# Last attention: the causal mask moves from TensorE to VectorE, rows over two PSUM banks, columns over two

## What is computed

```
def _L3_attn_ref(x, W1, b1, W2, b2):
    B, S, E = x.shape
    y = jnp.einsum('bse,ef->bsf', x, W1) + b1
    y = y.reshape(B, S, H, -1).transpose(0, 2, 1, 3)
    q, k, v = jnp.split(y, 3, axis=-1)
    w = jnp.einsum('bhqd,bhkd->bhqk', q, k) / dk
    mask = jnp.tril(jnp.ones((S, S), dtype=x.dtype))
    w = w * mask - NEG_BIG * (1.0 - mask)
    w = jax.nn.softmax(w, axis=-1)
    attn = jnp.einsum('bhqk,bhkd->bhqd', w, v)
...
    return jnp.einsum('bse,ef->bsf', attn, W2) + b2
```

## Time and profile before

| | |
|---|---|
| median of 3 runs | 1892.53 us (1886.91 to 1892.79) |
| profiled execution | 1895.08 us, its span 1893.3 us |
| busy TensorE, weight load, VectorE, ScalarE, GpSimd | 88, 73, 71, 58, 57% of the span |
| row maxima of the last attention that go into XNT (L2193) | 256, mean 502 ns |
| mean granted TensorE clock | 0.947 of full speed |

### The profile page before, as it was taken

How to read it: one execution, slowest core, us unless ns; L and a number is a source line. 1 busy time by engine, 2 the same in 40 slices (tenths; PEclk the granted TensorE clock), 3 DMA queues, 4 the chain that set the end, 5 groups by cost and what they waited for, 6 DMA issues and landing times. The chain is left out here.

```text
span 1893.3 us, 33635 instructions
## 1 busy us (share of the span) xinstructions
PE 1666.8 (88%) x12948; PEld 1385.3 (73%) x12976; DVE 1335.2 (71%) x2744; ACT 1090.4 (58%) x2240; POOL 1081.8 (57%) x1029
## 2 busy tenths in 40 slices
PE   6999999999999999999956888955898468999997
PEld 4888888888888888877855677844687356666676
DVE  6888888888888888743363477677577588777772
ACT  3677776667676767654544555632433345666666
POOL 4888899999999999980054455644177510101011
PEclk9999999999999999999968999966999788999999
DMA  3000000000100000000014200030165200000000
GB/s 93 15 1 15 1 6 10 2 15 1 38 1 1 2 1 1 1 28 0 1 56 141 71 11 2 2 95 0 35 149 129 54 1 1 1 2 2 1 2 24
DMA packets 57839, 47.92 MB, mean 25 GB/s; under 512 B 8384, under 2 KB 49504, under 8 KB 57552
## 3 DMA queue, kind: packets, MB, share of 16 engines
q1 hardware_dynamic: 48128, 32.92, 5.9%
q0 software_dynamic: 8496, 12.33, 3.0%
q10 hardware_dynamic: 1056, 0.52, 0.1%
HBM read 36.45 MB, written 9.31 MB: 24 GB/s over the span
## 5 line engine op out<-in xcount | busy, mean ns | idle before, releaser
L750 POOL TENSOR_TENSOR dtl<-dts,dth 128x512 fp32r<-128x512 f32 x256 | 350.1, 1368 | 20.5
L680 DVE TENSOR_REDUCE nm<-PS 128x1 f32<-128x1024 f32 x256 | 311.3, 1216 | 24.3 <-PE PS L200 23.1
L2032 ACT ACTIVATE ET_a<-PS 128x256 f32<-128x256 f32 (+2 forms) x512 | 222.6, 493 | 125.5 <-PE PS L1945 78.8
L748 POOL CAST dth<-dts 128x512 fp32r<-128x512 f32 x256 | 237.1, 926 | 52.8 <-ACT dts L607 51.7
L198 PE MATMUL PS<-xh,yh 128*128 128x512 f32 x512 | 225.2, 440 | 10.5 <-ACT XNT L600 5.3
L1843 POOL TENSOR_SCALAR_AFFINE_SELECT ET_a<-ET_a 128x1024 f32<-128x1024 f32 x32 | 34.9, 1092 | 310.4 <-ACT ET_a L2032 310.4
L141 PE MATMUL PS<-C,XN 128*128 128x128 f32 x1120 | 176.4, 283 | 38.3 <-POOL W4h L1121 22.7
L200 PE MATMUL PS<-xh,yl 128*128 128x512 f32 x512 | 204.2, 399 | 0.0
L199 PE MATMUL PS<-xl,yh 128*128 128x512 f32 x512 | 204.0, 398 | 0.0
L600 ACT ACTIVATE XNT<-PS,nm 128x1024 f32<-128x1024 f32 x128 | 142.7, 1115 | 80.9 <-DVE nm L680 80.2
L607 ACT ACTIVATE dts<-PS 128x512 f32<-128x512 f32 x256 | 152.5, 597 | 46.7 <-POOL dtl L750 44.0
(11 more groups left out here) (430 smaller groups left out, 4378.3 us busy)
## 6 DMA issues: line engine op xcount, KB each, us to landing
e_wg<-in_WgT SPq DMA_DIRECT2D x16, 256.0 KB
e_wu<-in_WuT SPq DMA_DIRECT2D x16, 256.0 KB
e_wd<-in_WdT SPq DMA_DIRECT2D x16, 256.0 KB
m_x_rows<-m_xs SPq DMA_DIRECT2D x1, 1472.0 KB, 5.1
m_xs<-m_x_rows SPq DMA_DIRECT2D x5, 256.0 KB
m_y_rows<-m_xs SPq DMA_DIRECT2D x5, 256.0 KB, 2.8
X<-in_L_attn_X SPq DMA_DIRECT2D x2, 512.0 KB, 4.6
wqn<-in_L_attn_Wq SPq DMA_DIRECT2D x8, 128.0 KB, 2.1
```

Of the source, the lines that this page charges most:

```text
L680: e.tensor_reduce(self.nm[:, half, i:i + 1], self.S[half], AX.X, MAX, negate=True).then_inc(*self.top.up((g, half)))
L748: e.tensor_copy(hi, src).then_inc(*ts.up((g, g4, "h")))
L750: e.tensor_tensor(lo, src, f(hi), SUB).then_inc(*ts.up((g, g4, "l")))
L2032: e.activation(dst, src, ACT.Exp, scale=self.SC, bias=0.0).then_inc(*self.ex.up(it))
```

## The change

The mask is no longer added by matmuls. GpSimd makes a bf16 tile `mk` of 1024 columns, zero but for the causal block in its last 128. For each query tile VectorE runs one `tensor_tensor_reduce` over 128 to 1024 columns: it adds the last columns of `mk` to the scores, multiplies by -1, writes the result back to PSUM and takes the minimum, that is the negated maximum. The instruction is followed by an accumulator read of 128x1. Tiles 4 to 7 lie in two neighbouring banks, filled by two matmuls of up to 512 columns (the second of 256 at least), and `P2` and the joining minimum go. Row tiles stand at places 0, 1, 2, 3, 4, 6, 8, 10 instead of 0 to 11. Tiles 0 to 3 use banks 0 to 3, tiles 4 to 7 the pairs 0-1 and 2-3 in turn, in all heads; columns use banks 4 and 5 while there are rows. A part waits for the readers of all its banks.

```
-        self.at = {(3 * j if kind == 1 else j): j for j in range(self.nr)}
+        self.col_at = {(3 * j if kind == 1 else j): j for j in range(self.nc_)}
+        self.row_at = {3 * j: j for j in range(4)} if kind == 1 else dict(zip((0, 1, 2, 3, 4, 6, 8, 10), range(8)))
...
-        rs, cs, rn, cn = list(range(3 if kind == 1 else 6)), [], 0, 0
+        rs, cs, rn, cn = [0, 1, 2], [], 0, 0
...
+        def put(it, banks):
+            self.bank_of[it] = banks[0], len(banks)
+            self.before[it] = [u for u in dict.fromkeys(last.get(b) for b in banks) if u]
+            for b in banks:
+                last[b] = it
         for x in range(NH + 8):
             if x == 5:
-                rs, cs, rn, cn = [0, 1, 2], [3, 4, 5], 0, 0
+                cs, rn, cn = [4, 5] if kind == 3 else [3, 4, 5], 0, 0
             elif x == NH:
                 cs, cn = list(range(4)), 0
...
+                    if kind == 3:
+                        put(it, [j] if j < 4 else [2 * (j % 2), 2 * (j % 2) + 1])
...
             if self.kind == 3:
-                i, c0, c1, first = self.rparts[j]
-                wd = max(c1 - c0, 256)
-                t = e.matmul(o[:, 0:wd], qs[:, 128 * i:128 * i + 128], kh[:, c0:c0 + wd], start=True, stop=first)
-                if not first:
-                    t = e.matmul(o[:, c1 - c0 - 128:c1 - c0], w.identb[:, :], w.mk[:, 0, 0:128], start=False, stop=True)
+                for c0 in range(0, 128 * j + 128, 512):
+                    wd = max(min(128 * j + 128 - c0, 512), 256)
+                    t = e.matmul(o[:, c0:c0 + wd], qs[:, 128 * j:128 * j + 128], kh[:, c0:c0 + wd], start=True, stop=True)
...
-                i, c0, c1, first = self.rparts[j]
-                dst = self.P2[:, n % 2, i - 4, hh:hh + 1] if first else M[:, i, col]
-                e.tensor_reduce(dst, o[:, 0:c1 - c0], AX.X, MAX, negate=True).then_inc(*self.top.up(it))
-                if j == self.nr - 1:
-                    m4 = M[:, 4:8, col].rearrange("p i c -> p (i c)")
-                    q.wait_ge(self.top, it)
-                    e.tensor_tensor(m4, m4, self.P2[:, n % 2, :, hh], MIN).then_inc(*self.top.up(("both", x)))
+                if j == 0:
+                    q.wait_ge(w.ready, "mask")
+                wd = 128 * j + 128
+                e.tensor_tensor_reduce(out=o[:, 0:wd], in0=o[:, 0:wd], in1=w.mk[:, 1024 - wd:1024], scale=-1.0, scalar=3e38, op0=ADD, op1=MIN,
+                                       accum_out=M[:, j, col]).then_inc(*self.top.up(it))
...
-            e.tensor_copy(self.mk[:, 0, 0:128], k.cst("caus")).then_inc(*ready.up("mask"))
+            e.memset(self.mk[:, 0:896], 0.0).then_inc(*ready.up("open"))
+            e.tensor_copy(self.mk[:, 896:1024], k.cst("caus")).then_inc(*ready.up("mask"))
```

More of the change, by code:

```diff
@@ L1088, in __init__ @@
         ops += ["one"] if kind == 3 else ["bq0", "one"]
-        ops += [("bm", 0), ("bm", 1), "ident"] + ([("mask", i, j) for i in range(3) for j in range(2)] if kind == 1 else ["mask"]) + ["va1", "va0"]
+        ops += [("bm", 0), ("bm", 1)] + (["ident"] + [("mask", i, j) for i in range(3) for j in range(2)] if kind == 1 else ["open", "mask"]) + ["va1", "va0"]
         self.ready = k.sig("s_weights", ops)
@@ L1629, in __init__ @@
         if kind == 3:
-            self.rparts, self.cparts = [], []
+            self.cparts = []
             for i in range(8):
-                w_ = 128 * (i + 1)
-                cut = 0 if w_ <= 512 else (384 if w_ == 640 else 512)
-                self.rparts += [(i, 0, cut, True)] * (cut > 0) + [(i, cut, w_, False)]
                 lo = 128 * i
@@ L1639, in __init__ @@
         else:
-            self.rparts, self.cparts = list(range(4)), list(range(4))
-        self.nr, self.nc_ = len(self.rparts), len(self.cparts)
+            self.cparts = list(range(4))
+        self.nr, self.nc_ = 8 if kind == 3 else 4, len(self.cparts)
         self.avs = [self.av_of(x) for x in range(NH)]
@@ L1688, in __init__ @@
         last = {b: first[b] for b in range(3 if kind == 1 else 4)}
-        rs, cs, rn, cn = list(range(3 if kind == 1 else 6)), [], 0, 0
+        rs, cs, rn, cn = [0, 1, 2], [], 0, 0
         rows, cols = [], []
+        def put(it, banks):
[3 more added lines that the diff above has]
+                last[b] = it
         for x in range(NH + 8):
             if x == 5:
-                rs, cs, rn, cn = [0, 1, 2], [3, 4, 5], 0, 0
+                cs, rn, cn = [4, 5] if kind == 3 else [3, 4, 5], 0, 0
             elif x == NH:
                 cs, cn = list(range(4)), 0
[L1696 to L1699, removed]
-                    cols.append(it)
-                if x < NH:
-                    b, rn, it = rs[rn % len(rs)], rn + 1, ("row", x, self.at[place])
-                    self.bank_of[it], self.before[it], last[b] = b, last.get(b), it
+            for place in range(14):
+                if place in self.col_at and 0 <= x - 5 < NH:
+                    it = ("col", x - 5, self.col_at[place])
+                    put(it, [cs[cn % len(cs)]])
+                    cn += 1
+                    cols.append(it)
+                if place in self.row_at and x < NH:
+                    it, j = ("row", x, self.row_at[place]), self.row_at[place]
+                    if kind == 3:
+                        put(it, [j] if j < 4 else [2 * (j % 2), 2 * (j % 2) + 1])
+                    else:
+                        put(it, [rs[rn % 3]])
+                    rn += 1
                     rows.append(it)
@@ L1733, in __init__ @@
         self.row = k.sig("a_row", rows)
-        self.top = k.sig("a_row_max", [y for r in rows for y in ([r] + ([("both", r[1])] if kind == 3 and r[2] == self.nr - 1 else []))])
+        self.top = k.sig("a_row_max", rows)
         self.col = k.sig("a_col", cols)
@@ L1792, in bank_free @@
     def bank_free(self, q, it):
[L1793 to L1802, removed]
+        for a in self.before[it]:
+            if a[0] == "project":
+                q.wait_ge(self.mi, a)
+            elif a[0] == "row":
+                q.wait_ge(self.top, a)
+            else:
+                q.wait_ge(self.ex, a)
+        return self.k.bank(*self.bank_of[it])
     def steps(self):
@@ L1867, in maxima @@
             _, n, c = u
-            q.wait_ge(self.top, ("both", 4 * n + 3) if self.kind == 3 else ("row", 4 * n + 3, self.nr - 1))
+            q.wait_ge(self.top, ("row", 4 * n + 3, self.nr - 1))
             for j in range(4):
@@ L1975, in pe @@
                 self.moe.pe_at(e, q, x, j, self)
[L1976 to L1979, removed]
+            if j in self.col_at and 0 <= x - 5 < self.NH:
+                col(x - 5, self.col_at[j])
+            if j in self.row_at and x < self.NH:
+                row(x, self.row_at[j])
             if j in self.AV_AT and 0 <= x - 6 < self.NH:
@@ L2017, in col @@
             it = ("col", x, j)
-            o = k.bank(self.bank_of[it])
+            o = k.bank(*self.bank_of[it])
             if x >= 2:
@@ L2207, in dve @@
         for x, j in self.steps():
-            if j in self.at and x < self.NH:
-                row(x, self.at[j])
+            if j in self.row_at and x < self.NH:
+                row(x, self.row_at[j])
             if (x, j) in self.misc:
```

10 lines of the change are left out of this document (5 added, 5 removed).

## The result

Over four runs of each the median went from 1891.86 us (1886.91 to 1892.79) to 1922.65 us (1918.76 to 1925.23). The ratio is 1.017, with a 95% interval of 1.0156 to 1.0185: slower by 31 us, where 1914 us was forecast. The layers ahead of the last attention are the same code but for the mask tile, and still differ from one profiled execution to the next: the last attention begins (at VectorE's memset of `ET`) at 1526.78 us before and at 1521.56 after.

The account below looks back on a forecast made before the run. VectorE was taken to bound the first five heads, TensorE heads without side jobs; `project` heads also wait. Column-bank waits and the first heads' cost summed to +21 us on the 1892.5 us median: 1914 us, range 1890 to 1928.

Parts of the forecast that it names:

- first five heads: Last attention's opening heads, only row jobs, VectorE setting the pace: longer operations and fewer row banks cost +3 us in all.
- x = 5 and 6: First two heads with rows and columns side by side, both with `project`: longer waits cost +2.1 us.
- five repetitions: Five rounds of four heads, rows and columns side by side: +2.7 us a round, +13.7 in all.
- x = 27 to 31: Last heads with rows: 27, 29, 30 and 31, without `project`, cost +2.5 us together, 28 nothing.
- heads with `project`: Column part 4 waits 3 us for an exp behind the K copies: 12.8 against 11.65, 13.2 against 12.20 us.
- The waits for two column banks: Main term: column j waits for the exp of column j-2, not j-3; four heads take +2.7 us.
- the walk: Step-by-step timing of TensorE's matmuls in the overlapped heads with two column banks: four heads at 8.8, 9.2, 12.8, 13.2 us.
- The credit for the mask matmuls: TensorE in each head loses eight mask matmuls of 0.12 us, 0.96 us; net 0.9 us less work.
- "nothing else moved" figure: TensorE's saved work over the 27 heads where rows and columns share it would give 25 us.
- Rival A: Overlapped heads: TensorE stays the bound, exps keep up, mask savings decide: -22 us, 1871 us; chance 0.12.
- VectorE: Row maxima with the new operation take 5.9 to 6.6 us a head against 5.8 before: VectorE gains nothing.
- Rival C: VectorE's new operation takes two cycles a column, 10.7 us a head: +85 us, 1978 us; chance 0.05.

Follow-up runs that it names:

- run 3: The changed kernel with eleven useless 512-column matmuls ahead of column part 4 in the twelve heads with `project`: 1914.59 us, ratio 1.011.
- run 1: The kernel before with two column banks instead of three from head 5 on, masks and row parts unchanged: 1930.34 us, ratio 1.0191.
- run 5: The changed kernel with the mask added by matmuls again and plain reductions on VectorE, banks as in the change: 1927.17 us, ratio 1.0201.
- run 2: The kernel before with only the mask moved to VectorE's new operation on each tile's last row part, banks unchanged: 1886.96 us, ratio 0.9963.
- Run 7: The kernel before with the mask operation on VectorE and ScalarE's K copies behind exps 2 and 3, three column banks: 1870.01 us, ratio 0.9896.
- run 4: The changed kernel with ScalarE's two K copies of the first `project` put behind exps 2 and 3: 1897.71 us, ratio 1.0009.
- run 6: The kernel before with ScalarE's two K copies put behind exps 2 and 3, nothing else: 1880.09 us, ratio 0.9946.

## Why the prediction was right, and where a size was off

The sign, the stage, the engine and the wait were as forecast; the median came out 8.7 us above the forecast. The clock was in no term and in no rival of the prediction. In stages of the two profiled executions:

| term | predicted | measured | with the clock held (run 3) |
|---|---|---|---|
| first five heads | +3 | +1.8 | +1.8 |
| x = 5 and 6 | +2.1 | +3.2 | +1.6 |
| five repetitions | +13.7 | +23.9 | +13.2 |
| x = 27 to 31 | +2.5 | +2.3 | +2.3 |
| last five heads | 0 | 0 | 0 |
| sum | +21 | +31 | +19 |

With the clock held the sum would have been +19, so the prediction's other terms were 2 us too high together; this covered some of what the clock added, by luck.

**The term that was mis-sized** is the heads with `project`, put at "12.8 against 11.65, +1.1" and "13.2 against 12.20, +1.0". They measured 13.05 to 14.89. The 3 us wait at column part 4 was priced by its length alone, as if TensorE went on at full speed after it. The clock falls to the 1.2 GHz level for part of what follows the wait, in nine of the ten such heads of the repetitions. In the five repetitions that is 10.7 us (230.03 against 219.33), at x = 5 and 6 another 1.6: the 12 us between the last two columns. The four-head row at 13.61 and 14.00, run 1's pair at 13.03 and 13.96, and run 3 show it in three ways.

**The waits for two column banks.** The turn of a bank, 1.19 us, carried the walk. TensorE's timeline of the head without side jobs, from 1643.81, has:

```profile
1646.25 0.50 PE L1951 MATMUL PS<-QS_a,KH_a 128*128 128x512 f32 x1
...
1647.44 0.44 PE L1951 MATMUL PS<-QS_a,KH_a 128*128 128x384 f32 x1 [0.22 <-ACT ET_a L2038]
...
1649.28 0.50 PE L1951 MATMUL PS<-QS_a,KH_a 128*128 128x512 f32 x1
```

Column parts 4 and 6 start 2.44 and 3.63 us into the head and the first sums end at 5.47, to the hundredth as in the walk. The whole is 8.77 for 8.78 measured without side jobs, 9.2 for 9.37 with `give` (the 0.4 counted for `give` was 0.6), 12.8 and 13.2 for 12.66 and 13.06 with the clock held. Runs 1 and 5 show that this alone makes the loss. The Trainium skill ("Perfetto Trace Analysis", Matmuls) advises to rotate independent matmuls through different PSUM banks, so that the evacuation of one overlaps the next matmuls. The trace agrees, and adds how many: a part takes TensorE some 0.35 us and its bank 1.19, so that two banks are too few and three just do.

**The credit for the mask matmuls.** 0.12 us each was right where TensorE sets the pace: 0.48 against 0.35 from pair to pair. But run 2 got 0.4 us of the 0.96 a head, by its timelines since ScalarE's exps became the next limit. The prediction's "nothing else moved" figure of 25 us was thus not to be had even with three banks. Rival A's 1871 us needed a bank turn under 0.8 us; there was none. Run 7 comes to that time in another way, with a third column bank and the chain of the K copies moved.

**VectorE.** Forecast were 5.9 to 6.6 us a head. From start to start a 128-column operation of after takes 0.25 us and the others mostly N x 1.04 ns and 0.08 to 0.12 more: with 4608 columns and eight operations 5.4 to 5.8 us, no more than before. The 0.14 for the accumulator read was counted and lies beside the next operation. Rival C is out: 1024 columns take 1.15 us, about 1.1 ns a column and as much as a reduction, not twice that. The Trainium skill's rule of half throughput ("Vector Engine (DVE) Microarchitecture Reference", Points easy to get wrong) was read rightly as not reaching this case.

**The first five heads** cost +1.8 us for a forecast of +3, for other reasons. Run 2, with the operation and six banks, has 49.26 us there and run 5, with the row banks of after and reductions, 49.07; before has 49.16. So neither half costs anything alone. Against run 5 the kernel after has 1.9 us more. The view of busy time by stretch has for these heads of run 5:

```profile
1519.98:1569.05 49.07, 31.84 (x132) 19.79 (x133) 42.66 (x66) 16.57 (x25) 7.35 (x9) 0.83 0.00 0
```

VectorE is busy for 42.66 us there and for 44.39 in after, so 1.7 of the 1.9 us are its own work; its idle time grows by 0.2 only (6.6 against 6.4). VectorE's groups by shape from 1535 to 1572 us show where, first in after:

```profile
L2200 DVE CUSTOM_DVE_ANT_0 PS<-PS,mk 128x896 f32<-128x896 f32 x5 | 5.6, 1124 | 0.0
...
L2200 DVE CUSTOM_DVE_ANT_0 PS<-PS,mk 128x1024 f32<-128x1024 f32 x4 | 4.9, 1233 | 1.0 <-PE PS L1930 1.0
```

The same groups in run 5:

```profile
L2199 DVE TENSOR_REDUCE XNT<-PS 128x1 f32<-128x1024 f32 x5 | 6.1, 1218 | 0.4 <-PE PS L1932 0.4
L2199 DVE TENSOR_REDUCE XNT<-PS 128x1 f32<-128x896 f32 x5 | 5.4, 1084 | 0.0
```

Over the seven sizes from 256 up the operation is 6 to 47 ns longer than the reduction, 0.2 us a head or 1.0 in five. That is the larger part; what makes the rest of the 1.7 was not followed up. TensorE's clock is lower there in after, 0.67 against 0.83. No run held it, but where rows have six banks it hardly counts: before has 49.15 us at 0.76, and run 1, with the same code in these heads, 49.01 at 0.90.

**Nothing hidden came out.** x = 27 to 31 and the last five heads came as forecast. Rows waited for VectorE's maxima for 7.1 us in all, up to 1.4 us at a time, but 6.9 of it in the first five heads; from 1597 to 1790 us the view of waits has none, and there the walk priced them at nothing.

Why the clock falls after some of these waits and not after others of the same length (run 1's head of 13.03 us has one of 2.66, and a head of after with one of 2.84 takes 13.05 us at 1.00) the runs do not settle.

## What to carry to other kernels

Count how long a buffer takes from the first write until it is free again, and divide by the number of buffers: that, and not the busy share of its reader, says whether the producer waits. When a walk gives the matmul engine a new wait of microseconds in the middle of a busy stretch, price the clock behind it as well as the wait, or look for what stands in the reader's queue ahead of the instruction that is waited for; moving two copies behind two exps was worth 25 us of the median here, and 32 in the last attention of the profiled executions. A change with two halves should be run as halves: here the half that pays was hidden behind the one that costs.

## What the runs showed of the hardware

- TensorE's granted clock fell from the 2.4 to the 1.2 GHz level behind many, not all, waits of 2.7 to 2.9 us in a stretch where it was otherwise busy (mean 0.66 between one and the next sums), at 0 to 2.2 us a head, 1.07 on average over ten. Eleven useless matmuls in the wait kept it at 1.00 and made the head 0.95 us shorter. With waits of at most 0.6 us (run 4) it stayed at 1.00 too.
- VectorE's operation of add and minimum, in place over two PSUM banks, with a bf16 mask from SBUF, takes 1.02 ns for each further column (128x1024: 1235 ns; 128x512: 714 ns), and the accumulator read of 138 ns behind it is hidden when the next operation is ready. The Trainium skill ("VectorE: DVE Perf Modes", The DRAIN you can't avoid) has the next operation wait until the pipe is empty, and adds that one that is not held starts earlier. No run here shows when the pipe is empty; the next operation began 0.64 us after the start of one of 0.73 us, together with that one's accumulator read.
- In the first five heads, where VectorE sets TensorE's pace, TensorE's mean clock differed between executions of the same code: 0.76, 0.90 and 0.83 with mask matmuls on six banks (before, runs 1 and 6), 0.69 and 0.76 without them (runs 2 and 7). On the banks of after it was 0.67 without them (after, runs 3 and 4) and 0.83 with them (run 5).
- A bf16 matmul of 128 columns costs 0.12 us in a row of 512-column matmuls. Of this 0.08 is the longer gap behind the matmul after it (0.32 us for 0.24 in the earlier trace rows). In the timeline of the weight loads before, the load for the row at 1639.89 starts only at 1639.66 and takes 0.19 us, so the row waits for its weights.
